# Loading the opening of a four-stage network in pieces: x by chunks, projections into four banks, FFN weights during attention, token rows by two transfers

## The reference

```
x = x + ln(linear_attention(ln(x)))        # 16 heads, running state over all rows
x = x + ln(ffn(ln(x)))                     # 256 -> 1024 -> 256, with low-rank additions
x = x + ln(two_mamba_layers(ln(x)))
x = x + ln(mixture_of_8_experts_top2(ln(x)))
```

```
lt = x[:, 1:17];  even = lt[:, ::2];  odd = lt[:, 1::2]
m1 = (even[:, :4, :, None] * odd[:, :4, None, :]).reshape(B, 1024, 256)
m2 = (even[:, 4:, :, None] * odd[:, 4:, None, :]).reshape(B, 256, 1024)
h   = gelu(x @ W1.T + scale * x @ m1.T + b1)
out = h @ W2.T + scale * h @ m2.T + b2
```

## Time and profile before

| | |
|---|---|
| median of 3 runs | 4020.06 us (4019.51 to 4025.07) |
| the profiled execution | 4023.78 us |
| its span, first to last instruction | 4022.0 us |
| first block and transfers of x | 0 to 17.8 us |
| attention, from its first load to the last write of x | 17.8 to 446.5 us |
| FFN, from its first load to the first product of its loop | 450.7 to 495.3 us |
| mean granted clock of TensorE over the span | 0.894 of full speed |

### The profile page before, as it was taken

One profiled execution on the slowest core, in us unless ns is written; L12 is line 12 of the kernel. 1 busy time (PEld: TensorE's weight loads), 2 busy tenths in 40 slices (PEclk: granted clock), 3 DMA queues, 4 the chain that ended last, 5 costly groups with the idle time before them and its releaser, 6 DMA issues. The chain is left out here.

```text
span 4022.0 us, 67053 instructions
## 1 busy us (share of the span) xinstructions
PE 3267.0 (81%) x20668; PEld 2263.8 (56%) x20669; DVE 2538.1 (63%) x3759; ACT 1942.4 (48%) x4180; POOL 2075.5 (52%) x1328
## 2 busy tenths in 40 slices
PE   5999699269888988989938999898998843899970
PEld 3777566145555555555515555555555533788860
DVE  2656323547777777777736777777777767554545
ACT  1222022057666666666526766767667633233320
POOL 0000000137677777777725777877778765222216
PEclk8888699689999999999969999999999965899995
DMA  1000000113223222232212232322323234111113
GB/s 55 1 0 0 23 0 0 62 39 84 55 58 80 53 66 71 56 74 63 60 36 63 56 83 55 79 59 62 75 55 83 57 123 138 51 47 47 47 45 110
DMA packets 151616, 228.30 MB, mean 57 GB/s; under 512 B 25250, under 2 KB 84034, under 8 KB 149700
## 3 DMA queue, kind: packets, MB, share of 16 engines
q1 hardware_dynamic: 143300, 202.30, 18.7%
q0 software_dynamic: 8064, 23.08, 2.0%
HBM read 119.99 MB, written 23.59 MB: 36 GB/s over the span
## 5 line engine op out<-in xcount | busy, mean ns | idle before, releaser
L943 POOL TENSOR_TENSOR m_hc<-m_h,m_Cb 128x1024 f32<-128x1024 f32 x512 | 1234.5, 2415 | 413.0 <-PE m_bank L1354 255.3
L1080 DVE TENSOR_TENSOR_SCAN m_h<-m_dA,m_vel 128x1024 f32<-128x1024 f32 x512 | 1169.1, 2283 | 93.0 <-ACT m_dA L1220 50.0
L1354 PE MATMUL m_bank<-m_hc,ident 128*128 128x512 f32 x2048 | 1055.1, 630 | 102.4 <-POOL m_hc L943 102.1
L1220 ACT ACTIVATE m_dA<-m_delta,m_rate 128x255 f32<-128x255 f32 x2048 | 874.1, 497 | 46.2 <-DVE m_h L1080 26.0
L1370 PE MATMUL m_vel<-m_M,m_U 128*128 128x128 bf16 x4096 | 542.9, 222 | 76.1 <-DVE m_h L1080 58.3
L1354 PEld LDWEIGHTS m_bank<-m_hc,ident 128*128 128x128 f32 x2048 | 362.1, 197 | 323.2 <-issue 222.5
L1372 PE MATMUL m_vel<-m_M,m_U 112*128 112x128 bf16 x4096 | 542.7, 222 | 0.0
L1370 PEld LDWEIGHTS m_vel<-m_M,m_U 128*128 128x128 bf16 x4096 | 403.0, 99 | 211.1 <-DVE m_h L1080 102.2
L1372 PEld LDWEIGHTS m_vel<-m_M,m_U 112*128 112x128 bf16 x4096 | 407.0, 99 | 82.1 <-issue 70.3
L1284 PE MATMUL m_bank<-m_pair,m_in 128*128 128x256 f32 x1024 | 280.1, 401 | 68.8 <-DVE m_cv L1020 63.1
L1069 DVE TENSOR_TENSOR m_vel<-m_vel,m_entry 128x4 f32<-128x4 f32 x512 | 82.5, 161 | 366.8 <-PE m_vel L1372 363.8
(11 more groups left out here) (281 smaller groups left out, 5570.5 us busy)
## 6 DMA issues: line engine op xcount, KB each, us to landing
m_Cb<-m_c_rows SPq DMA_DIRECT2D x256, 256.0 KB, 3.2
m_M<-m_Mhi SPq DMA_DIRECT2D x128, 256.0 KB, 4.3
m_M<-m_Mlo SPq DMA_DIRECT2D x64, 256.0 KB, 3.9
m_U<-m_Uhi SPq DMA_DIRECT2D x128, 128.0 KB, 3.2
y_rows<-x_y SPq DMA_DIRECT2D x40, 256.0 KB, 2.1
m_U<-m_Ulo SPq DMA_DIRECT2D x64, 128.0 KB, 3.3
g_stage<-in_e_w SPq DMA_DIRECT2D x8, 1024.0 KB, 5.5
o_stage<-in_e_w SPq DMA_DIRECT2D x16, 512.0 KB, 4.2
```

Of the source, the lines that this page charges most:

```text
L943: nc.gpsimd.tensor_tensor(hc[:, g].rearrange("p m a t -> p m (a t)"), h[:, p % 2, 2 * g:2 * g + 2].rearrange("p m a t -> p m (a t)"), Cb[: ...
L1080: nc.vector.tensor_tensor_scan(flat(h), flat(dA), VB[:, 2 * g * 512:2 * (g + 1) * 512], 0.0, ALU.mult, ALU.add).then_inc(s["scan_done"], 1)
L1220: nc.scalar.activation(dA[:, p % 2, m, a, 1:CM], delta[:, par, m, 1:CM], ACT.Exp, scale=rate[:, m, NG * p + a:NG * p + a + 1]).then_inc(s[ ...
L1354: last = nc.tensor.matmul(Y[g][:], net.ident[:], hc[:, g, :, a, :], start=(p == 0 and a == 0), stop=(p == NPAIR - 1 and a == NG - 1))
```

## The change

- The first block issues x's first chunk (512 rows) and the identity, and waits for neither. Each has a semaphore of its own: `x_in[0]`, `ident_in`.
- SP issues, behind the attention's six loads, the other seven chunks of x (one semaphore each) and then the FFN's five loads. The FFN's weights have tiles of their own for both phases (`FfnWeights`).
- DVE waits for `x_in[i]` before a chunk's statistics and for `loaded` only after the first chunk is normalised; PE waits for `ident_in` first and for `loaded` behind the transposes; ACT waits for `loaded` behind the first chunk's exponentials.
- The first chunk's four projections go to the four banks S, without waits between them. DVE's `stats(1)` stands behind the third feature, and `normal(1)` behind the masks.
- The 16 token rows go to a buffer in HBM (`tok_rows`) by one transfer and come back into one partition by a second, which waits for the first.
- m2 is made by 8 products of 256 columns; the column order changes, with DVE's adds to match: bank 4 + i now holds all 8 blocks of 64 columns of product i.

The core of the diff:

```diff
@@ attention_phase, sync
                 sp.dma_start(parity[:], dram["parity"]).then_inc(loaded, 16)
+                for c in range(1, NCH):
+                    tiles = slice(c * TPC, (c + 1) * TPC)
+                    sp.dma_start(net.x[:, tiles, :], net.x_rows[:, tiles, :]).then_inc(net.x_in[c], 16)
+                net.ffn.load(sp, dram)
@@ attention_phase, vector
                 nc.vector.memset(vt[:], 1.0).then_inc(ones_set, 1)
-                dve.wait_ge(loaded, LOADS)
 
                 def stats(i):
+                    if isinstance(i, int):
+                        dve.wait_ge(net.x_in[i], 16)
...
                 stats(0)
                 normal(0)
-                stats(1)
+                dve.wait_ge(loaded, LOADS)
                 for g in range(4):
-                    feature(0, 0, g)
+                    dve.wait_ge(qk_exp, 1 + g + 1)
+                    nc.vector.scalar_tensor_tensor(phi[:, 0, g, :], S[g][:], 0.0, exps[:, g % 2, :],
+                                                   ALU.max, ALU.add).then_inc(phi_done, 1)
+                    if g == 2:
+                        stats(1)
+                masks(0, 0)
                 normal(1)
-                masks(0, 0)
                 chunk(0, 0, True, True)
                 chunk(1, 1, True, True)
+                for c in range(4, NCH):
+                    dve.wait_ge(net.x_in[c], 16)
@@ attention_phase, scalar
-                act.wait_ge(loaded, LOADS)
...
                 for g in range(4):
-                    expo(0, g)
+                    expo(0, g, S[g])
+                act.wait_ge(loaded, LOADS)
+                act.wait_ge(ones_set, 1 + 1)
                 masked(0, 0)
@@ attention_phase, tensor
-                pe.wait_ge(loaded, LOADS)
+                pe.wait_ge(net.ident_in, 16)
...
                 for k in range(KD):
                     turn(0, 0, k)
+                pe.wait_ge(loaded, LOADS)
+                pe.wait_ge(xT_done, 1 + KD)
                 for g in range(4):
-                    project(0, 0, g)
+                    for k in range(KD):
+                        last = nc.tensor.matmul(S[g][:], wqkv[:, k, g * P:(g + 1) * P], xT[:, 0, k, :],
+                                                start=(k == 0), stop=(k == KD - 1))
+                    last.then_inc(qk_psum, 1)
@@ ffn_phase, sync
-                sp.dma_start(w1[:], dram["f_w1"]).then_inc(loaded, 16)
...
                 sp.wait_ge(first_done, 1 + 1)
-                for r in range(4 * RANK1):
-                    sp.dma_start(tok[:, r, :], xn[1 + r:2 + r, 0, :]).then_inc(tok_done, 16)
+                sp.dma_start(tok_rows, xn[1:1 + 4 * RANK1, 0, :]).then_inc(tok_kept, 16)
+                sp.wait_ge(tok_kept, 16)
+                sp.dma_start(tok[0:1].rearrange("p r d -> p (r d)"), tok_rows.rearrange("r d -> (r d)").unsqueeze(0)).then_inc(tok_done, 16)
@@ ffn_phase, vector
-                for q in range(4):
-                    w = w2[:, 2 * q:2 * q + 2, :]
-                    last = nc.vector.scalar_tensor_tensor(w, B[4 + q][:].rearrange("p (k o) -> p k o", k=2),
+                for i in range(RANK1):
+                    w = w2[:, :, i * (D // 4):(i + 1) * (D // 4)]
+                    last = nc.vector.scalar_tensor_tensor(w, B[4 + i][:].rearrange("p (k o) -> p k o", k=KH),
                                                           scale[:, 0:1], w, ALU.mult, ALU.add)
@@ ffn_phase, tensor
-                for m in range(KH):
-                    r, half = m // 2, m % 2
-                    for i in range(RANK1):
-                        col = (m % 2) * D + i * (D // 4)
-                        last = nc.tensor.matmul(B[4 + m // 2][:, col:col + D // 4],
-                                                tok[0:1, 2 * (RANK1 + i) + 1, half * P:(half + 1) * P],
-                                                tok[0:1, 2 * (RANK1 + i), r:D:4], start=True, stop=True)
+                for i in range(RANK1):
+                    for half in range(2):
+                        to = B[4 + i][:].rearrange("p (r a o) -> p a r o", a=2, o=D // 4)[:, half]
+                        of = tok[0:1, 2 * (RANK1 + i), :].rearrange("p (o r) -> p r o", r=4)
+                        last = nc.tensor.matmul(to, tok[0:1, 2 * (RANK1 + i) + 1, half * P:(half + 1) * P], of,
+                                                start=True, stop=True)
@@ build, sync
-                sp.dma_start(net.x, dram["x"].rearrange("(n p) d -> p n d", p=P)).then_inc(stored, 16)
-                sp.dma_start(net.ident[:], dram["ident"]).then_inc(stored, 16)
-                sp.wait_ge(stored, 32)
+                sp.dma_start(net.x[:, 0:TPC, :], net.x_rows[:, 0:TPC, :]).then_inc(net.x_in[0], 16)
+                sp.dma_start(net.ident[:], dram["ident"]).then_inc(net.ident_in, 16)
```

More of the change, by code:

```diff
@@ L65, in __init__ @@
         self.own_pool = ctx.enter_context(nc.semaphore("own_pool"))
+        self.x_rows = dram["x"].rearrange("(n p) d -> p n d", p=P)
+        self.x_in = [ctx.enter_context(nc.semaphore(f"x_in{c}")) for c in range(NCH)]
+        self.ident_in = ctx.enter_context(nc.semaphore("ident_in"))
     def sb(self, ctx, name, shape, dt=F32):
@@ L103, in _, with __init__, load @@
                         sp.sem_clear(used)
+class FfnWeights:
+    LOADS = 5 * 16
+    def __init__(self, net, ctx):
+        self.w1 = net.sb(ctx, "f_w1", [P, KD, HID])
+        self.w2 = net.sb(ctx, "f_w2", [P, KH, D])
+        self.b1 = net.sb(ctx, "f_b1", [P, KH])
+        self.b2 = net.sb(ctx, "f_b2", [P, D])
+        self.scale = net.sb(ctx, "f_scale", [P, 1])
+        self.loaded = ctx.enter_context(net.nc.semaphore("f_loaded"))
+    def load(self, sp, dram):
+        sp.dma_start(self.w1[:], dram["f_w1"]).then_inc(self.loaded, 16)
+        sp.dma_start(self.w2[:], dram["f_w2"]).then_inc(self.loaded, 16)
+        sp.dma_start(self.b1[:], dram["f_b1"]).then_inc(self.loaded, 16)
+        sp.dma_start(self.b2[:], dram["f_b2"].partition_broadcast(P)).then_inc(self.loaded, 16)
+        sp.dma_start(self.scale[:], dram["f_scale"].partition_broadcast(P)).then_inc(self.loaded, 16)
 def inverse_root(net, pool, out, variance):
@@ L326, in turned, with expo @@
                     nc.scalar.copy(xT[:, par, k, :], HEAD[:]).then_inc(xT_done, 1)
-                def expo(i, g):
+                def expo(i, g, bank=HEAD):
                     act.wait_ge(qk_psum, 1 + i * 4 + g + 1)
-                    nc.scalar.activation(negs[:, g % 2, :], HEAD[:], ACT.Relu, scale=-1.0).then_inc(qk_neg, 1)
+                    nc.scalar.activation(negs[:, g % 2, :], bank[:], ACT.Relu, scale=-1.0).then_inc(qk_neg, 1)
                     act.wait_ge(qk_neg, 1 + i * 4 + g + 1)
@@ L501, in ffn_phase @@
         B = net.banks(ctx, "f_bank")
-        loaded, tok_done = net.own("f_loaded"), net.own("f_tok_done")
+        loaded, tok_done, tok_kept = net.ffn.loaded, net.own("f_tok_done"), net.own("f_tok_kept")
+        net.sems.append(loaded)
+        tok_rows = nc.dram_tensor("tok_rows", (4 * RANK1, D), F32, kind="Internal").ap()
         own_dve = net.own("f_own_dve")
@@ L511, in ffn_phase @@
                                            net.sem("f_z_rstd"))
-        LOADS = 5 * 16
+        LOADS = net.ffn.LOADS
         net.start()
@@ L2185, in _ @@
             def _(sp):
-                sp.dma_start(net.x, dram["x"].rearrange("(n p) d -> p n d", p=P)).then_inc(stored, 16)
-                sp.dma_start(net.ident[:], dram["ident"]).then_inc(stored, 16)
-                sp.wait_ge(stored, 32)
+                sp.dma_start(net.x[:, 0:TPC, :], net.x_rows[:, 0:TPC, :]).then_inc(net.x_in[0], 16)
+                sp.dma_start(net.ident[:], dram["ident"]).then_inc(net.ident_in, 16)
+        with ExitStack() as weights:
+            net.ffn = FfnWeights(net, weights)
+            net.run(attention_phase)
+            net.run(ffn_phase)
         for phase in phases:
-            if phase in (mamba_phases, moe_phases):
-                phase(net)
-            else:
-                net.run(phase)
+            phase(net)
 def layout(a):
```

18 lines of the change are left out of this document (4 added, 14 removed).

## The result

The changed kernel takes **3954.3 us** (median of 4 runs, 3952.9 to 3957.53) beside 4019.78 us for the kernel before (4 runs, 4015.5 to 4025.07): 65.5 us less, ratio 0.9838, 95% interval 0.9821 to 0.9855. The forecast was 3977, the range 3969 to 3993. The profiled execution took 3957.53 us (span 3955.7) against 4023.78 (span 4022.0), 66.3 us less.

The account below looks back on a forecast made before the run. The kernel was taken as a chain of non-overlapping stages, bound in the touched openings by waits and serial work. Gains 18.5 + 9.5 + 1.5 + 7.0 + 6.8 = 43.3 us, so 4020.06 - 43.3 = 3976.8; range 3969 to 3993.

Parts of the forecast that it names:

- the first one: Whole kernel: stages form a chain, so only touched places can change and each microsecond saved there counts in full.
- 3 us for fetched instructions: Opening: instruction fetches share the transfers' engines; up to 3 us lost, allowed in the range only, worst case 3993.7.
- the rival for instructions: Opening: first chunk, six loads or engines' instructions arrive late among other transfers; 5.6 us lost, 3982.4, chance 0.08.
- Start: Kernel's start: no waits on SP, so everything up to the projections moves 18.5 us earlier, bounds 17.3 and 18.7.
- Projections: Attention's opening: four projection groups follow each other without gaps, 12.75 us instead of 22.25, a gain of 9.5.
- First tile: Attention's first tile, behind the projections: a warmer PE clock gains 1.5 us, bounds 0 and 4.8.
- Token rows: FFN's opening: two transfers instead of sixteen, 4.6 us instead of 11.6, a gain of 7.0, bounds 5.9 and 7.5.
- m2: FFN's opening: 16 records of 256 columns take 7.2 us instead of 13.98, a gain of 6.8, lower bound 0.
- The stepped read: Rival on m2: reading with a step of four elements costs its whole gain, giving 3983.6 us; chance 0.2.
- The clock didn't stay low: Rival on the opening: clock stays low, projections gain 6.2 and nothing behind them, giving 3981.6 us; chance 0.17.
- The rival with cold tiles: Attention's later tiles: more fall to the lower clock, around 5 us each; 14 more give 4047 us; chance 0.02.

Follow-up runs that it names:

- e6: Kernel before with five more already reached waits on VectorE, its code ahead of the layers 3 instructions longer: 3984.35 us beside 4017.21, ratio 0.9917.
- e12: Kernel before with one more already reached wait on VectorE, its code 1 instruction longer: 4015.59 us beside 4016.95, one execution.
- e1: Kernel before with only m2's 8 wide products in place of its 32 narrow ones: 4025.79 us beside 4019.04, ratio 1.0019.
- e5: Changed kernel plus 24 tiny TensorE products behind both Mamba layers, in the gating stage: 3954.53 us, ratio 0.9842.
- e7: Changed kernel with 12 already reached waits added on SP, lengthening its code ahead of the layers: 3957.14 us, ratio 0.9846.
- e8: Changed kernel with ACT's wait for the memset ones back ahead of its first copy: 3959.41 us, one execution.
- e9: Changed kernel with the first chunk's four projections in one bank again, each waiting for the feature before it: 3969.02 us, one execution.
- e4: Changed kernel plus 24 tiny TensorE products at the opening of the second Mamba layer only: 3937.64 us, ratio 0.9801.
- e10: Changed kernel with the FFN's five loads issued at the FFN's opening again, ahead of the token transfers: 3953.89 us, one execution.
- e2: Changed kernel with m2's 32 narrow products back in place of the 8 wide ones: 3943.69 us, ratio 0.9812.
- e3: Changed kernel plus 24 tiny TensorE products at the attention's opening: 3942.82 us, ratio 0.9804.

## Why the prediction was wrong

The step that failed is the first one: "Only the places that the diff touches can change", and with it "a microsecond taken from the attention's or the FFN's opening is taken from the whole". The argument looked at data and semaphores, and on those it was right: the stages meet at their blocks, and nothing of x or the weights reaches into the Mamba layers differently. But the engines' code is one stream through all stages, and an edit that makes it longer or shorter moves every later loop in it. I had allowed 3 us for fetched instructions, as a loss, in the opening. It was 41.4 us of gain in the first layer and 16.7 us of loss in the second, 24.7 us net; 4.4 more (+3.7 and +0.7) were lost between the stages. The first is mostly VectorE's: e6, with VectorE's program alone, shows 37.5 of it (and e12 that one instruction isn't enough), and the rest goes with TensorE's shorter program (e1). The second is TensorE's alone (e1 to e5), and e7 excludes SP's. No rival named this; the rival for instructions was about their arrival in the first 15 us.

The numbers of the places that are touched, term by term:

- *Start*: 18.5, bounds 17.3 to 18.7; measured 20.1, outside the bounds. The statistics began at 5.14, where 5.3 was forecast, a shift of 18.74. The 1.3 beyond is ACT's table load, which I hadn't looked at: before, it stood behind two waits and so in front of the first copy; e8 gives it back. The wait for the six loads was covered, as said.
- *Projections*: 9.5; measured 10.7, and 10.8 against e9 (9.5 to 9.9 by the 12.5 to 12.8 us of e4, e5 and e7). The form was right (some slow records, then the higher rate): 8.89 us of records beside 9.3 in the sum, a wait of 2.65 beside 2.8, and the 0.65 that I had put on top for one or two more slow records wasn't needed here, though in e4, e5 and e7 it was (12.75 forecast). `stats(1)` did delay the third feature's successor, since the records no longer hid it.
- *First tile*: 1.5; measured 2.7, with the clock at 0.70 instead of 0.51. The narrow halves took 3.03 and 3.44. In e4, e5 and e7 the tile took 17.0 to 17.1, which leaves 0.6 of this term. Projections and first tile together: 11.0 forecast, 13.4 between the two profiled executions, 10.1 to 10.4 from the same before to e4, e5 and e7. How near these two terms came is in part luck of the execution.
- *Token rows*: 7.0, best bound 7.5; measured 7.8. The way out took 1.43 from issue to issue and the way in 2.39 to PE's start, so the 0.9 us that I had added for waits and issues is inside the rows' times already. That the weights' early loads count for nothing by themselves but are needed for this (e10) I had only half seen: I counted their issue on SP, and not that the transfers themselves would stand in the small transfers' way, 5.0 us by e10.
- *m2*: 6.8, bounds 0 and 6.8; measured 6.3. 16 records took 7.43 beside m1's 7.19. **The stepped read costs 0.24 us at most**, so that rival is out for this kernel. The Trainium skill ("SBUF — State Buffer", section "Door 1: The DMA port swizzle (why `[64,N]` ≈ `[32,N]`)") says that each access that crosses to a new line of 16 bytes pays a penalty. At a pace of 0.46 us for 256 columns, at a granted clock of 0.50, no such price is to be seen here; at the upper level it wasn't measured.
- The FFN's first pass took 16.94 instead of 16.09, 0.85 us given back.
- The clock didn't stay low, and the attention's later part didn't change (mean clock 0.85, 0.6 us longer). The rival with cold tiles fell as well.

The five terms measured 47.6 where 43.3 was forecast, and 46.1 with what was given back. Had everything else stayed, the profiled time would have been 4023.8 - 46.1 = 3977.7, inside the range. The range was made from the terms alone, and held no term for what the edit does to the rest of the program.

The Trainium skill does state the mechanism, in "Runtime: NRT & Kernel Launch", section "Instruction fetch mechanics": code is prefetched in sequence, and a taken branch to a target outside what is held stops the engine until it has been fetched. The traces agree: in the slow placements VectorE's branch back is followed by a stop of 2.7 to 3.0 us and TensorE's lasts 3.3 to 4.0, and packets of instructions move meanwhile. The same section calls the crossing of a block's boundary mostly hidden. The second stops, 2.2 to 3.0 us on VectorE and 2.65 to 3.10 on TensorE, are not hidden here. They come soon after a branch back, and e12 puts VectorE's at a fixed place of the code, as a boundary would be; that it is one is not shown.

**Open.** Whether two instructions on VectorE would already be enough, and where the step lies on TensorE, between -23 and +1. Why 61 packets on q8 cost 17 to 21 us in the second layer and only 2 to 8 in the first is in part answered by the records. In both layers the branch back then lasts 3.3 to 4.0 us. But the second layer alone has TensorE's second stop, 13.2 to 15.6 us in all; the first layer of before, e2, e3, e6 and e12 has none. Likely the products issued before the branch cover the first stop and nothing is left to cover the second; no run tried it. The 3.7 us between the FFN and the first scan are in the profiled executions of the changed kernel (130.5) and of e1 (129.6), and in none of the twelve others (126.3 to 127.4), among them e4 and e5, which have exactly the changed kernel's code up to that scan. So they belong to the execution, not to the change.

## What to carry to other kernels

When an edit adds or removes instructions ahead of a long loop, count them per engine, and compare the period of the loops that were *not* touched and the packets of the instruction queues in them, before crediting or blaming the edit. If a loop's period alternates with its back edge, look at what the engine's sequencer did right behind the branch; a few idle instructions ahead of it are worth one run: here 3 instructions on VectorE gave 33 us, and 24 small products on TensorE 17. And of two edits that each give little, such as the early loads and the short path of the token rows, the pair can give most of it.

## What the runs showed of the hardware

- Three instructions that do nothing, ahead of a loop on VectorE, made the program 33 us shorter (e6), one did nothing (e12).
- In the slow placement VectorE stood still for 2.7 to 3.0 us behind its branch back and for 2.2 to 3.0 us two instructions later (before), one instruction later in e12. TensorE's branch back lasted 3.3 to 4.0 us in every layer with 61 packets on q8 and 0.2 in every layer with 15 or 16, and in the second layer a stop of 2.65 to 3.10 us followed 0.5 us after its end (after).
- q14's packets here have 0.96 MB / 117 = 8.2 KB, q8's 1.72 / 105 = 16.4 KB; q14's count followed VectorE's place, q8's TensorE's.
- A one-partition fp32 operand of 256 columns, read with a step of four elements, takes 0.46 us beside 0.45 without the step, at a granted clock of 0.50.
- 16 KB go from SBUF to HBM and back into one partition in 3.3 to 3.9 us from the tile to the first product, and in 8.9 with the weights' transfers under way (e10).
- ACT's table load of 1.28 us came at once with one wait ahead of the first copy (4.23 us, after), and behind the waits with two (11.31, e8).
- The granted clock is printed as 1.00 for 13 to 25 us, though the first four or five records of the projections there go at the lower level's rate.
